# GpSimd writes one column of a spare tile between every two gathers, in the attention stage and in the last stage of a graph network

## The chip, the cores and the metric

The kernel runs on one core of one Trainium2 chip. The metric is the device time of one execution in microseconds (us), lower is better. The chip's profiler gives one further, profiled execution, from which every row below comes. Short names of the engines, as the rows have them: PE is TensorE (matmuls; PEld is its weight load), DVE is VectorE, ACT is ScalarE, POOL is GpSimd, SP is SyncE.

## What is computed

The input is 6,250 nodes with 256 features and a list of 106,250 edges (source, destination) sorted by destination. The reference has two layers. Each has a graph part, a linear attention part and an expert part:

```
xn = layernorm(x)
x  = x + gcn(xn, src, dst) + mix0(xn)              # layer 0
x  = x + experts0(layernorm(x))
xn = layernorm(x)
x  = x + gat(xn, edge_index) + mix1(xn)            # layer 1: graph attention, 8 heads of 32
x  = x + experts1(layernorm(x), router_edges)      # router = a small graph attention, 4 experts
```

The two parts that matter here are graph attentions. For every edge they compute

```
e     = leaky_relu(a_src[src] + a_dst[dst])
ex    = exp(e - m[dst])
out   = segment_sum(ex * h[src], dst) / segment_sum(ex, dst)
```

In the first (the attention stage) h has 8 heads of 32 columns. In the second (the router of the last stage) h has 4 heads of 4 columns, and the edge list has 131,072 entries. The router's result picks 2 of 4 experts for each node; each expert is a 256 to 512 to 256 network with a GELU, weighted by the gate.

## The kernel before, in words

Nodes stand 128 to a window, 49 windows (W). Edges stand 128 to a slot, sorted by window. `Stage2` (the attention stage, from line 2286) works through 880 slots of edges, `Stage3` (the last stage, from line 2934) through 1,072. Both take the slots in groups of four (GROUP): 220 groups and 268 groups. All loops are unrolled; each engine has its own hand-written program (`sync`, `pool`, `tensor`, `scalar`, `vector`), and semaphores tie them together.

For one group q the work is:

- **GpSimd** (`pool`, lines 2430 and 3101) issues four gathers (lines 2438 and 3108). One gather is an indirect DMA that fetches 128 rows of a table in HBM, one for each edge of the slot: rows of 264 float32 in the attention stage, of 20 float32 in the last stage. They land in the buffer `rows`, which has room for 8 groups in the attention stage and for 10 in the last stage (ROWS). Before it fills a buffer again, GpSimd waits until that buffer's group is used up: in the attention stage for the four matmuls of the group eight back (`s_sum`), in the last stage for the split of the group ten back (`s_part`, raised by DVE at line 3306). GpSimd has nothing else to do in either stage.
- **SyncE** loads the destinations of the group, spread over the partitions (`st_bc`).
- **ACT** makes a transposed one-hot matrix of the destinations (lines 2551 and 2555; 3191 and 3195), and the exponentials (lines 2573, 2574; 3202).
- **PE** multiplies the one-hot matrix with the window's `a_dst` (lines 2457 and 3127, into `st_pad`), and later the one-hot matrix with the weighted rows (lines 2468 and 3138, into `st_po`). These last matmuls are the segment sums.
- **DVE** adds `a_src` and `a_dst` (lines 2637 to 2647; 3279 to 3289), makes the one-hot matrix (2626; 3268), adds the four segment sums to the window's sum (line 2678; line 3314), and weights the gathered rows (line 2655; line 3298). In the last stage it also splits the weighted rows into three bf16 parts (lines 3303 to 3306).

DVE's order in a group is: exponents of group q+2, one-hot of group q+5, the four additions of group q, message of group q+2. PE's order is: the sums of group q, then a share of other dense work, then the scores of group q+3. The dense work of the attention stage is the keys, values and output of the linear attention; that of the last stage is the experts, which a planner (`plan`) spreads over groups 23 to 261. DVE takes the experts' results from PSUM at lines 3381 and 3394.

An earlier stage, `Stage1`, gathers in the same way (line 1455) and is not changed. Small `memset`s on GpSimd stand at the program's start, and one directly behind the last gather of the stage before `Stage1` (line 1016, in `block_mask`).

Of the kernel before, what the change touches and what calls it, by code (L numbers as in the profile page):

```python
# [15 lines left out]
P = 128  # L16
# [43 lines left out]
class Phase:  # L60


    def __init__(self, nc, tag, side="left"):
        self.nc, self.tag, self.ctx, self.sems, self.side = nc, tag, ExitStack(), [], side
# [194 lines left out]
class Prelude:  # L259
# [110 lines left out]
    def pool(self, g):  # L370
        for q in range(self.GROUPS):
            b = q % self.ROWS
            if q >= self.ROWS:
                g.wait_ge(self.s_sum, q - self.ROWS + 1)
            for u in range(GROUP):
                t = GROUP * q + u
                g.indirect_dma_start(self.rows[:, b, u, :], None, self.R.tab0,
                                     bass.IndirectOffsetOnAxis(self.R.gsrc[:, t:t + 1], 0)).then_inc(self.s_rows[b], 16)
        block_mask(g, Steps(g, self.s_mask), self.R.ahead.diag, HC0)
# [634 lines left out]
def block_mask(g, st, tile, width):  # L1014

    st.then(g.memset(tile[:, :], 1.0))
    v = tile[:, :].rearrange("p (g e) -> p g e", e=width)
    n = P // width
    st.then(g.affine_select(out=v, in_=v, compare_op=ALU.is_ge, fill=0.0, base=0,
                            pattern=[[-width, n], [0, width]], channel_multiplier=1))  # L1020
    st.then(g.affine_select(out=v, in_=v, compare_op=ALU.is_ge, fill=0.0, base=width - 1,
                            pattern=[[width, n], [0, width]], channel_multiplier=-1))
# [1263 lines left out]
class Stage2:  # L2286
# [32 lines left out]
    def __init__(self, f, nc, R, A):  # L2319
        self.nc, self.R, self.A = nc, R, A  # L2320
        self.wkv = self.weights(R)
        at = C * self.KV
        self.rows = self.store(R, at, self.ROWS * GROUP * GROW).rearrange("p (b u d) -> p b u d", b=self.ROWS, u=GROUP)
        at += self.ROWS * GROUP * GROW
        self.kc = self.store(R, at, 2 * self.KV).rearrange("p (k n) -> p k n", k=2)
        at += 2 * self.KV
        assert at <= C * NP
        K = self.PAIRS
        old = self.wkv.rearrange("p c n -> p (c n)")
        self.wqt = old[:, 0:K * D].rearrange("p (k d) -> p k d", k=K)  # L2330
        self.wout = old[:, K * D:2 * K * D].rearrange("p (k d) -> p k d", k=K)
        old = self.kc.rearrange("p k n -> p (k n)")
        self.m1 = old[:, 0:K * D]
        self.bd = old[:, K * D:K * D + K * P].rearrange("p (k e) -> p k e", k=K)
        self.kvsum = old[:, K * D + K * P:K * D + 2 * K * P]
        assert 2 * K * D <= C * self.KV and K * D + 2 * K * P <= 2 * self.KV
        self.diag = f.sb("diag", [P, P])
        self.xtb = f.sb("xtb", [P, self.XTB, C, P])
        self.sq = f.sb("sq", [P, 2 * W * GH + 2 * HC1])
        self.square = self.sq[:, 2 * W * GH:].rearrange("p (k e) -> p k e", k=2)  # L2340
        self.hotb = f.sb("hotb", [P, self.HOTB, P, GROUP], BF16)
        self.bc = f.sb("bc", [P, self.BCB, GROUP * P], BF16)
        self.pcol = f.sb("pcol", [P, 2])
        self.far = f.sb("far", [P, 2, GROUP * P], BF16)
        self.count = f.sb("count", [P, P, GROUP], BF16)
        self.hott = f.sb("hott", [P, self.HOTT, GROUP, P], BF16)
        self.hot = f.sb("hot", [P, self.HOTF, GROUP, P])
        self.adl = f.sb("adl", [P, W, PARTS, 2 * GH], BF16)
        self.zd = f.sb("zd", [P, GROUP, 2 * GH])
        self.z = f.sb("z", [P, 2, GROUP, 2, GH])  # L2350
        self.lm = self.sq[:, 0:W * GH].rearrange("p (w h) -> p w h", h=GH)
        self.d = f.sb("d", [P, 2, GROUP, GH])
        self.z0 = self.sq[:, W * GH:2 * W * GH].rearrange("p (w h) -> p w h", h=GH)
        self.ssum = f.sb("ssum", [P, 2, 2, HEADS])
        self.var = f.sb("var", [P, HEADS])
        self.std = f.sb("std", [P, HEADS])
        self.rs = f.sb("rs", [P, HEADS])
        self.po = f.ps("po", [P, self.BANKS, 512])
        self.pkv = f.ps("pkv", [P, 512])
        self.pacc = f.ps("pacc", [P, 512])  # L2360
        self.pad = f.ps("pad", [P, GROUP, PARTS, 2 * GH])
        self.wps = f.ps("wps", [P, GROUP, GH])
        self.zero = f.sb("zero", [P, 512], BF16)
        self.brow = f.sb("brow", [2, D])
        self.s_st, self.s_count, self.s_lm, self.s_d0, self.s_e0, self.s_a0, self.s_zero = (
            f.sem(n) for n in ("st", "count", "lm", "d0", "e0", "a0", "zero"))
        self.s_rows = [f.sem(f"rows{b}") for b in range(self.ROWS)]
        self.s_bc = [f.sem(f"bc{b}") for b in range(self.BCB)]
        self.s_hot, self.s_tt, self.s_hb, self.s_ad, self.s_z, self.s_d, self.s_ex, self.s_msg = (
            f.sem(n) for n in ("hot", "tt", "hb", "ad", "z", "d", "ex", "msg"))  # L2370
        self.s_zd, self.s_far, self.s_col = (f.sem(n) for n in ("zd", "far", "col"))
        self.s_sum, self.s_acc = f.sem("sum"), f.sem("acc")
        self.s_fw, self.s_mask, self.s_kvs, self.s_bd, self.s_pm, self.s_m1, self.s_pw = (
            f.sem(n) for n in ("fw", "mask", "kvs", "bd", "pm", "m1", "pw"))
        self.s_weff, self.s_row, self.s_mix, self.s_mixed = (f.sem(n) for n in ("weff", "row", "mix", "mixed"))
        self.s_xt = [f.sem(f"xt{k}") for k in range(self.XTB)]
        self.s_kvp, self.s_kc, self.s_sq, self.s_var, self.s_std, self.s_k1, self.s_kv = (
            f.sem(n) for n in ("kvp", "kc", "sq", "var", "std", "k1", "kv"))
# [51 lines left out]
    def pool(self, g):  # L2430
        block_mask(g, Steps(g, self.s_mask), self.diag, HC1)
        for q in range(self.GROUPS):
            b = q % self.ROWS
            if q >= self.ROWS:
                g.wait_ge(self.s_sum, GROUP * (q - self.ROWS + 1))
            for u in range(GROUP):
                t = GROUP * q + u
                g.indirect_dma_start(self.rows[:, b, u, :], None, self.R.tab1,  # L2438
                                     bass.IndirectOffsetOnAxis(self.R.gsrc[:, t:t + 1], 0)).then_inc(self.s_rows[b], 16)

# [493 lines left out]
class Stage3:  # L2934
# [24 lines left out]
    def __init__(self, f, nc, R, A, out):  # L2959
# [37 lines left out]
            f.sem(n) for n in ("st", "count", "lm", "d0", "e0", "a0", "bias"))  # L2997
        self.s_rows = [f.sem(f"rows{b}") for b in range(self.ROWS)]
        self.s_bc = [f.sem(f"bc{b}") for b in range(self.BCB)]
        self.s_far, self.s_col = f.sem("far"), f.sem("col")  # L3000
        self.s_hot, self.s_tt, self.s_ad, self.s_zd, self.s_z, self.s_d, self.s_ex, self.s_msg, self.s_part = (
            f.sem(n) for n in ("hot", "tt", "ad", "zd", "z", "d", "ex", "msg", "part"))
# [98 lines left out]
    def pool(self, g):  # L3101
        for q in range(self.GROUPS):
            b = q % self.ROWS
            if q >= self.ROWS:
                g.wait_ge(self.s_part, q - self.ROWS + 1)
            for u in range(GROUP):
                t = GROUP * q + u
                g.indirect_dma_start(self.rows[:, b, u, :], None, self.R.tabr,  # L3108
                                     bass.IndirectOffsetOnAxis(self.R.rsrc[:, t:t + 1], 0)).then_inc(self.s_rows[b], 16)

# [534 lines left out]
```

## Time and profile before

| | us |
|---|---|
| three executions without the profiler | 4553.6, 4543.36, 4551.01 |
| their median | 4551.01 |
| the profiled execution, first to last instruction (the span) | 5387.9 |
| first gather of the attention stage to its last | 2100.2 to 3425.3 |
| first gather of the last stage to its last | 3545.5 to 5314.5 |

The page gives no other time of the profiled execution than its span. It is 837 us longer than the median of the executions without the profiler. Busy time is the time in which an engine executes; "idle before" is time in which it stood still before instructions of a group, with the one that released it. Where the trace finds no instruction as releaser it writes "issue", "remote", or the name of some DMA.

### The profile page before, as it was taken

What the parts mean: (1) busy time and instruction counts of PE and PEld (TensorE: products, weight loads), DVE (VectorE), ACT (ScalarE), POOL (GpSimd) and SP (SyncE); (2) the same over time, 40 slices, a digit from 0 to 9 for tenths busy, and PEclk for the clock granted to TensorE, in tenths of its full rate; (3) what the DMA queues carried; (4) which work ended last, traced back from release to release, by engine and by line L of the source; (5) the groups of instructions that cost most, each with busy time, mean ns of one, the idle gap of its engine ahead of it and who ended that gap; (6) DMA issues with size and microseconds to landing.
All of it is one profiled execution on the core that took longest, in us unless ns stands there. A gap on an engine that the chain in (4) does not pass through costs nothing. (4 is left out here: it accounts for less than half of the span.)

```text
span 5387.9 us, 67250 instructions
## 1 busy us (share of the span) xinstructions
PE 3828.0 (71%) x17777; PEld 2450.6 (45%) x17779; DVE 3145.7 (58%) x10032; ACT 2409.6 (45%) x5559; POOL 2781.9 (52%) x2880
## 2 busy tenths in 40 slices
PE   7587789889888995676777678522666666666663
PEld 7444455556555653344444445421433333333342
DVE  7564556454454655776767767734555555555556
ACT  6232222223222333787877633323444544444444
POOL 0362656565554103666666666446555555555552
PEclk9997999999999997989888888655788788787877
DMA  2322111111111005444444455231111111111111
GB/s 91 75 71 82 40 31 41 28 39 38 29 37 24 10 31 142 115 122 117 119 118 120 125 136 136 78 83 28 30 30 31 29 31 30 30 28 29 30 30 23
DMA packets 291737, 331.29 MB, mean 61 GB/s; under 512 B 80182, under 2 KB 246062, under 8 KB 291366
## 3 DMA queue, kind: packets, MB, share of 16 engines
q0 software_dynamic: 105328, 175.77, 15.2%
q1 hardware_dynamic: 186038, 151.23, 10.1%
q8 instruction: 153, 2.51, 0.2%
q14 instruction: 218, 1.79, 0.1%
HBM read 289.56 MB, written 30.77 MB: 59 GB/s over the span
## 5 line engine op out<-in xcount | busy, mean ns | idle before, releaser
L3108 POOL DMA_INDIRECT st_rows<-tabr,router_rsrc x1072 | 1022.6, 954 | 750.6 <-DVE st_part L3306 447.8
L2438 POOL DMA_INDIRECT all_XT<-tab,graph_gsrc x880 | 843.7, 959 | 482.6 <-issue 236.7
L1455 POOL DMA_INDIRECT st_rows<-tab,graph_gsrc x748 | 735.1, 983 | 570.1 <-PE st_pe L1478 299.1
L2468 PE MATMUL st_po<-all_XT,st_hot 128*128 128x264 f32 x1760 | 569.8, 471 | 152.8 <-issue 85.7
L1704 ACT ACTIVATE st_h<-st_ph,st_shift,st_scale 128x448 f32<-128x448 f32 x448 | 320.7, 724 | 733.7 <-PE st_ph L1566 519.9
L3165 PE MATMUL st_py<-st_w,st_hid 128*128 128x256 f32 x1568 | 527.2, 489 | 55.0 <-issue 50.9
L3127 PE MATMUL st_pad<-st_adr,st_hott 128*128 x1072 | 68.8, 177 | 678.7 <-DVE st_zd L3279 536.6
L2678 DVE TENSOR_TENSOR gat_sum<-gat_sum,st_po 128x264 f32 x880 | 376.2, 428 | 200.4 <-remote 79.6
L2468 PEld LDWEIGHTS st_po<-all_XT,st_hot 128*128 128x128 f32 x1760 | 343.7, 222 | 293.1 <-issue 200.0
L3165 PEld LDWEIGHTS st_py<-st_w,st_hid 128*128 128x128 f32 x1568 | 367.4, 247 | 124.2 <-issue 59.1
L3153 PE MATMUL st_px<-all_XT,st_w 128*128 128x512 f32 (+2 forms) x832 | 406.1, 635 | 18.3 <-ACT st_hid L3213 12.9
L3202 ACT ACTIVATE st_rows<-st_d 128x16 f32<-128x16 f32 x268 | 57.9, 216 | 785.2 <-DVE st_d L3289 603.2
L3127 PEld LDWEIGHTS st_pad<-st_adr,st_hott 128*128 128x128 bf16 x1072 | 51.2, 100 | 778.6 <-issue 771.1
L1579 PE MATMUL st_po<-all_XT,st_h 128*128 128x256 f32 x1568 | 374.9, 387 | 14.5 <-DVE all_X L1895 5.1
L1566 PE MATMUL st_ph<-st_h,all_XT 128*128 128x448 f32 x896 | 372.8, 566 | 13.5 <-ACT st_h L1704 11.8
L1566 PE MATMUL st_ph<-st_xt,all_XT 128*128 128x448 f32 x896 | 367.0, 560 | 18.5 <-ACT st_h L1704 17.4
L3314 DVE TENSOR_TENSOR router_racc<-router_racc,st_po 128x60 f32 x1072 | 230.4, 215 | 225.2 <-DMA all_XT<-in_m_wout 144.7
L1791 DVE TENSOR_TENSOR gcn_acc<-gcn_acc,st_pe 128x65 f32 x748 | 166.2, 222 | 332.5 <-PE st_pe L1478 223.7
L1579 PEld LDWEIGHTS st_po<-all_XT,st_h 128*128 128x128 f32 x1568 | 292.2, 192 | 68.1 <-issue 23.8
L2655 DVE TENSOR_TENSOR all_XT<-all_XT,st_wps 128x1024 f32<-128x1024 f32 x220 | 267.3, 1215 | 22.3 <-remote 21.5
L1895 DVE SCALAR_TENSOR_TENSOR all_X<-st_po,st_gate,all_X 128x256 f32 x392 | 169.5, 478 | 143.5 <-PE st_po L1579 89.7
L1566 PEld LDWEIGHTS st_ph<-st_h,all_XT 128*128 128x128 f32 x896 | 175.6, 201 | 168.9 <-issue 140.8
(517 smaller groups left out, 7453.3 us busy)
## 6 DMA issues: line engine op xcount, KB each, us to landing
st_bc<-drowr SPq DMA_DIRECT2D x268, 128.0 KB
st_bc<-drow SPq DMA_DIRECT2D x220, 128.0 KB
st_rows<-tabr,router_rsrc POOLq DMA_INDIRECT x1072
all_XT<-tab,graph_gsrc POOLq DMA_INDIRECT x880
st_xtb<-xtd SPq DMA_DIRECT2D x98, 128.0 KB
st_rows<-tab,graph_gsrc POOLq DMA_INDIRECT x748
tab<-gat_sum SPq DMA_DIRECT2D x7, 924.0 KB
xtd<-all_XT SPq DMA_DIRECT2D x49, 128.0 KB, 1.7
```

The lines of the kernel that those rows point to most:

```text
L1455: g.indirect_dma_start(self.rows[:, b, u, :], None, self.R.tab0, bass.IndirectOffsetOnAxis(self.R.gsrc[:, t:t + 1], 0)).then_inc(self.s_ro ...
L1566: mm = t.matmul(self.ph[:, m % 3, 0:HALF], (self.w1, self.w2)[l][:, e, i, fb * P:(fb + 1) * P], src[:, i, h * HALF:(h + 1) * HALF], start= ...
L1579: mm = t.matmul(self.po[:, q % 2, j - 2 * k, :], self.h2[:, i, j * P:(j + 1) * P], self.wo[:, e, i, :], start=(i == 0), stop=(i == C - 1))
L1704: a.activation((self.h1, self.h2)[l][:, fb, h * HALF:(h + 1) * HALF], self.ph[:, m % 3, 0:HALF], ACT.Relu, bias=self.shift[:, l, i:i + 1], ...
L2438: g.indirect_dma_start(self.rows[:, b, u, :], None, self.R.tab1, bass.IndirectOffsetOnAxis(self.R.gsrc[:, t:t + 1], 0)).then_inc(self.s_ro ...
L2468: t.matmul(self.po[:, m % self.BANKS, 0:GROW], self.hot[:, q % self.HOTF, u], self.rows[:, q % self.ROWS, u, :], start=True, stop=True).th ...
L2655: v.tensor_tensor(m, m, self.wps[:, :, :].unsqueeze(3).to_broadcast([P, GROUP, GH, GC]), ALU.mult)\
L2678: v.tensor_tensor(aw, aw, self.po[:, (GROUP * q + u) % self.BANKS, 0:GROW], ALU.add).then_inc(self.s_acc, 1)
L3108: g.indirect_dma_start(self.rows[:, b, u, :], None, self.R.tabr, bass.IndirectOffsetOnAxis(self.R.rsrc[:, t:t + 1], 0)).then_inc(self.s_ro ...
L3153: mm = t.matmul(self.px[:, i, 0:n * P], self.w1[:, e, c, fb * P:(fb + 1) * P], R.XT[:, c, r * P:(r + n) * P], start=(c == 0), stop=(c == C ...
L3165: t.matmul(self.py[:, m % 2, 0:D], self.hid[:, (E1 * u + e) % 2, fb, j * P:(j + 1) * P], self.w2[:, e, fb, :], start=(fb == 0), stop=False)
L3314: v.tensor_tensor(aw, aw, self.po[:, q % self.SUMB, u * n:(u + 1) * n], ALU.add).then_inc(self.s_acc, 1)
```

## The change

A tile `rest` of 128 partitions by 2 float32 and a semaphore `s_rest` are added to both stages. Before every gather but the first of its stage GpSimd writes zero into column 0 of `rest` and raises `s_rest`; from the second of these on it first waits until the one before has raised the semaphore. Nothing reads `rest`. `Stage2` has 879 of these writes, `Stage3` has 1,071.

```diff
@@ Stage2.__init__
+        self.rest = f.sb("rest", [P, 2])
+        self.s_rest = f.sem("rest")
@@ Stage2.pool
             for u in range(GROUP):
                 t = GROUP * q + u
+                if t:
+                    if t > 1:
+                        g.wait_ge(self.s_rest, t - 1)
+                    g.memset(self.rest[:, 0:1], 0.0).then_inc(self.s_rest, 1)
                 g.indirect_dma_start(self.rows[:, b, u, :], None, self.R.tab1,
                                      bass.IndirectOffsetOnAxis(self.R.gsrc[:, t:t + 1], 0)).then_inc(self.s_rows[b], 16)
@@ Stage3.__init__
+        self.rest = f.sb("rest", [P, 2])
+        self.s_rest = f.sem("rest")
@@ Stage3.pool
             for u in range(GROUP):
                 t = GROUP * q + u
+                if t:
+                    if t > 1:
+                        g.wait_ge(self.s_rest, t - 1)
+                    g.memset(self.rest[:, 0:1], 0.0).then_inc(self.s_rest, 1)
                 g.indirect_dma_start(self.rows[:, b, u, :], None, self.R.tabr,
                                      bass.IndirectOffsetOnAxis(self.R.rsrc[:, t:t + 1], 0)).then_inc(self.s_rows[b], 16)
```

## Rows read from the trace of the kernel before

**Rows 1.** The page's head: span, then busy time of each engine.

```profile
span 5387.9 us, 67250 instructions
PE 3828.0 (71%) x17777; PEld 2450.6 (45%) x17779; DVE 3145.7 (58%) x10032; ACT 2409.6 (45%) x5559; POOL 2781.9 (52%) x2880
```

**Rows 2.** Busy time by stretch: first the attention stage, then the last stage.

```profile
core 0: us, PE busy (x) PEld busy (x) DVE busy (x) ACT busy (x) POOL busy (x), PEclk, DMA share, GB/s
2100.00:3430.00 1330.00, 940.60 (x3683) 571.52 (x3684) 927.99 (x2254) 868.76 (x2899) 843.75 (x880) 0.85 0.46 122
3545.00:5330.00 1785.00, 1042.75 (x4677) 626.99 (x4678) 947.22 (x4096) 826.50 (x1245) 1022.60 (x1072) 0.77 0.18 32
```

**Rows 3.** GpSimd's groups by line, the two that the change touches.

```profile
L3108 POOL DMA_INDIRECT st_rows<-tabr,router_rsrc x1072 | 1022.6, 954 | 750.6 <-DVE st_part L3306 447.8 <-issue 299.6 <-POOLq L73 3.2
L2438 POOL DMA_INDIRECT all_XT<-tab,graph_gsrc x880 | 843.7, 959 | 482.6 <-issue 236.7 <-remote 144.3 <-PE st_po L2468 101.3
```

**Rows 4.** GpSimd's waits over the run: us in total, times, longest us.

```profile
POOL st_rows L3108 <- DVE st_part L3306: 447.8, 110, 8.9
POOL st_rows L3108 <- issue: 299.6, 961, 1.1
...
POOL all_XT L2438 <- issue: 236.7, 758, 2.0
POOL all_XT L2438 <- remote: 144.3, 72, 3.1
POOL all_XT L2438 <- PE st_po L2468: 101.3, 49, 5.5
```

**Rows 5.** Timeline of the last stage, 4474 to 4483: start, us, engine, line.

```profile
4474.86 0.94 POOL L3108 DMA_INDIRECT st_rows<-tabr,router_rsrc  x1 [0.30 <-issue]
4476.11 0.95 POOL L3108 DMA_INDIRECT st_rows<-tabr,router_rsrc  x1 [0.31 <-issue]
4477.36 0.95 POOL L3108 DMA_INDIRECT st_rows<-tabr,router_rsrc  x1 [0.30 <-issue]
4478.68 0.97 DVE L3314 TENSOR_TENSOR router_racc<-router_racc,st_po 128x60 f32 x4 [5.55 <-DMA all_XT<-in_m_wout]
...
4482.22 0.24 DVE L3306 TENSOR_TENSOR st_part<-st_rows,st_part 128x80 bf16<-128x80 f32 x1
...
4482.73 0.95 POOL L3108 DMA_INDIRECT st_rows<-tabr,router_rsrc  x1 [4.43 <-DVE st_part L3306]
```

**Rows 6.** The two gather lines: shortest, median and longest in ns; who waited for them.

```profile
L2438 POOL DMA_INDIRECT all_XT<-tab,graph_gsrc x880: 943/949/1684, 2100.2 to 3425.3; - x176
  DVE st_z L2641: 0.5, 1
...
L3108 POOL DMA_INDIRECT st_rows<-tabr,router_rsrc x1072: 942/947/1699, 3545.5 to 5314.5; - x179
  DVE st_z L3283: 6.1, 2
```

**Rows 7.** DVE's waits in the attention stage, 2100 to 3430: in total, times, longest.

```profile
DVE st_zd L2637 <- DMA xtd<-tab_xt: 80.4, 17, 17.5
DVE gat_sum L2678 <- remote: 79.6, 46, 3.5
DVE gat_sum L2678 <- PE st_po L2468: 39.9, 31, 2.9
DVE all_XT L2655 <- remote: 21.5, 13, 2.8
```

**Rows 8.** DVE's waits in the last stage, 3545 to 5330.

```profile
DVE router_racc L3314 <- DMA all_XT<-in_m_wout: 144.7, 31, 7.5
DVE all_XT L3394 <- DMA st_brow<-in_m_bout: 134.5, 34, 6.9
DVE st_zd L3279 <- remote: 102.3, 22, 9.4
DVE all_X L3381 <- DMA st_brow<-in_m_bout: 69.4, 17, 6.9
DVE router_racc L3314 <- DMA tab<-front_tabt: 21.9, 6, 4.3
```

**Rows 9.** GpSimd's timeline, small writes at the program's start.

```profile
0.32 0.10 POOL L3635 MEMSET const-float32-0.0<- 128x1 f32 x1 [0.32 <-issue]
0.35 0.10 POOL L3635 MEMSET const-float32-1.0<- 128x1 f32 x1
0.38 0.10 POOL L3635 MEMSET const-bfloat16-1.0<- 128x1 bf16 x1
0.41 0.10 POOL L3635 MEMSET const-uint8-127<- 128x1 uint8 x1
...
9.43 0.21 POOL L137 MEMSET all_ones<- 128x128 f32 x1
9.69 0.14 POOL L139 MEMSET all_mask<- 128x49 f32 x1
```

**Rows 10.** GpSimd's timeline, a write directly behind a gather.

```profile
420.43 0.94 POOL L377 DMA_INDIRECT pre_rows<-tab,graph_gsrc  x1 [0.30 <-issue]
421.37 0.23 POOL L1016 MEMSET fold_diag<- 128x128 f32 x1
```

**Rows 11.** GpSimd's timeline, a gather behind another operation.

```profile
2099.48 0.39 POOL L1021 TENSOR_SCALAR_AFFINE_SELECT st_diag<-st_diag 128x128 f32<-128x128 f32 x1
...
2100.17 1.37 POOL L2438 DMA_INDIRECT all_XT<-tab,graph_gsrc  x1 [0.30 <-POOL st_diag L1021]
2101.84 0.95 POOL L2438 DMA_INDIRECT all_XT<-tab,graph_gsrc  x1 [0.30 <-issue]
```

## The prediction

> **What bounds the kernel now.** I read the page's head first: no engine is busy all the time, PE leads with 71% and GpSimd stands at 52% [rows 1]. That is an average over unlike stages, so the next view is busy time by stretch, for the two stages that are changed. The busiest engines are PE and DVE in the attention stage (941 and 928 us of 1330), PE and GpSimd in the last (1043 and 1023 of 1785) [rows 2]. GpSimd's share has to be read with care, because a gather costs more than its busy time. Inside a run of gathers they start 1.25 us apart (4474.86, 4476.11, 4477.36), 0.95 us busy and 0.30 us of "issue" [rows 5], and 961 of 1072 and 758 of 880 gathers have such a gap and no other [rows 4]. The gathers alone therefore fill
>
> - attention stage: 880 x 1.25 = 1100 us of the 1325 from first to last gather [rows 6];
> - last stage: 1072 x 1.25 = 1340 us of 1769 [rows 6].
>
> What is left is real waiting for a free buffer: 144.3 + 101.3 = 246 us in the attention stage, 448 us in the last [rows 3, 4]. In the profiled execution GpSimd is thus ahead of its consumers in both stages, and hardly anyone waits for a gather: 0.5 us and 6.1 us in all [rows 6].
>
> What makes the consumers slow there? The timeline shows one case: DVE stands for 5.55 us before line 3314, then the split at 3306 frees a buffer, and GpSimd, which had to wait 4.43 us, goes on [rows 5]. The view of DVE's waits collects these: 80.4 + 79.6 + 39.9 + 21.5 = 221 us in the attention stage [rows 7], 144.7 + 134.5 + 102.3 + 69.4 + 21.9 = 473 us in the last [rows 8]. All but 39.9 us of it has no believable releaser ("remote", or a DMA long done).
>
> **Profiled and timed execution.** This is the choice on which my number rests. The span is 5387.9 us and the median of the runs is 4551, so 837 us are in the profiled execution alone. DVE's unexplained waits of these two stages are 221 + 473 = 694 us, near enough to suspect that they are most of it. A gather's 1.25 us, in contrast, is the same in both stages and all but free of spread (median 949 and 947 ns, shortest 943 and 942) [rows 6], so I take it as the price without the profiler too. Two bounds for a timed run then follow.
>
> - (a) Time shrinks evenly, by 4551 / 5387.9 = 0.845: attention stage 1325 x 0.845 = 1120, last stage 1769 x 0.845 = 1495. GpSimd's slack is 1120 - 1100 = 20 us and 1495 - 1340 = 155 us.
> - (b) The unexplained waits go: 1325 - 221 = 1104 and 1769 - 473 = 1296, the latter lifted to GpSimd's 1340. Slack 4 us and 0.
>
> In both, most of the slack that the profile shows is not there in the time that counts.
>
> **The change, part by part.** Nothing is removed or moved. Added on GpSimd are 879 and 1071 writes of 128x1, each with an increment, and all but the first with a wait. No DMA is added, and no other engine has new work.
>
> *The wait* is for the write before the previous gather. GpSimd executes in order, so it is long done. Cost nothing; where the wait for a free buffer stands ahead of it, two waits come together, once in four gathers, and I cost that at nothing too, since it passes in the 0.30 us before a gather.
>
> *The write.* A 128x1 write takes 0.10 us [rows 9]. The trace has one write directly behind a gather: the gather starts at 420.43, lasts 0.94, and the write starts at 421.37, so no gap arises behind a gather [rows 10]. And it has a gather behind another operation: it starts 0.30 us after the end, as between two gathers [rows 11]. So the 0.30 us belongs to the gather that follows and isn't paid twice. The start spacing becomes 1.25 + 0.10 = 1.35 us. Bounds: at least 0.03 us, the spacing at which the four first writes start [rows 9] (the write would then run inside the 0.30 us), and below that nothing; at most the write, the 0.05 us that lie between dependent operations (9.43 + 0.21 to 9.69 [rows 9]), widened to 0.07, and a second 0.30 us, 0.47 in all. I take 0.10, because the rows of both neighbours (behind a gather, before a gather) are here.
>
> *The sum.* GpSimd needs 880 x 1.35 = 1188 us and 1072 x 1.35 = 1447 us.
>
> - By (a): 1188 - 1120 = +68 in the attention stage; 1447 is below 1495, +0. Sum +68.
> - By (b): 1188 - 1104 = +84; 1447 - 1340 = +107. Sum +191.
>
> I take the middle, +130: **4551 + 130 = 4681 us**. Against the profiled execution the same writes are 88 + 107 us, less than its slack of 246 + 448, so its span should grow little (under 60 us). The profile will show less than the timed runs do.
>
> *A rule against the row.* The write at 421.37 starts no earlier than its gather's end [rows 10], which is why I charge it in full. The Trainium skill (GPSIMD Engine Reference, section Instruction dispatch) says that completion doesn't hold back the next instruction: each of the eight cores starts it when its own share of the one before is done; and the same page says that two of the cores generate a DMA's descriptors. By that, six cores would write under the running gather, and two would still have it behind it. The rival "nearly free" below is what this would give; the row at 421.37 doesn't bear it out.
>
> **The rivals.**
>
> *Nearly free write.* The write runs inside the 0.30 us before the gather, 0.03 us each [rows 9]. GpSimd needs 880 x 1.28 = 1126 and 1072 x 1.28 = 1372: +6 by (a), +22 + 32 = +54 by (b). Middle +30: 4581. For it: small writes overlap in [rows 9]. Against: nothing shows a gather's 0.30 us overlapping with anything, 0.30 stands after a gather and after another operation alike [rows 11].
>
> *Hidden.* The slack of the profile (246 and 448 us [rows 4]) is there in the timed run too: 88 and 107 us vanish in it, 4551. That needs the 837 us to be spread where GpSimd doesn't mind, or a gather that takes less than 1.25 us without the profiler (at 1.10, even (b) hides the write in the last stage: 1072 x 1.20 = 1286 under 1296). For it: nobody waits for a gather in the trace [rows 6]. Against: slack of 246 of 1325 us isn't compatible with a run that is 15% shorter, unless the earlier stages lose nearly all of the 837.
>
> *Faster.* The waits of DVE have no named releaser. If they are no artefact, but PE's or a transfer's trouble with bursts of gathers, pacing the bursts shortens them. One eighth of the 694 us of [rows 7, 8] would be -87 us: 4464. It decides only while GpSimd has slack, and it must win more than the +68 to +191. Against: the waits are longer in the last stage, where DMA is busy 18% and a gather brings 128 rows of 80 bytes, 10 KB, than in the attention stage with 46% [rows 2]; contention would be the other way round. The gathers themselves aren't stretched either (medians 6 ns over the shortest).
>
> *Dear write.* The two-sided gap, 0.47 us a write: 880 x 1.72 = 1514 and 1072 x 1.72 = 1844. By (a) +394 + 349 = +743, by (b) +914. Around 5380. Against: [rows 10], no gap behind a gather.
>
> **How the numbers follow.** Forecast (0.10 us charged, GpSimd the bound in one or both stages) 0.50; nearly free 0.17; hidden 0.13; faster 0.12; dear 0.08. A measurement of this kernel can tell about 0.2%, 9 us, from no change. Same: all of hidden, and 0.04 of nearly free, where (a) gives 6 us: 0.17. Slower: 0.50 + 0.13 + 0.08 = 0.71. Faster 0.12. The forecast's own range is 4619 to 4742 by (a) and (b), and with a write of 0.17 us (the 0.07 included) up to 880 x 1.42 - 1104 + 1072 x 1.42 - 1340 = +328, 4879. The range takes this in at the top and hidden at the bottom, less the runs' own spread of 10 us: 4540 to 4880. Left out are faster and dear, together 0.20.
>
> **What would show it.** Right: a MEMSET row x879 and x1071 at about 100 ns; gathers in a run start 1.35 us apart, and still show 0.30 us of "issue"; GpSimd's waits for line 3306 and for 2468/"remote" shrink by about 107 and 88 us; the profiled span grows by far less than the median of the runs. Wrong: a start spacing of 1.28 or less (nearly free) or over 1.5 (dear); an unchanged median with 1.35 us spacing (the timed run has slack, hidden); DVE's unexplained waits under 600 us in sum (faster). If DVE begins to wait for gathers at line 2641 or 3283, the bound moved as forecast, only later.

## The result: 9 us slower, 0.24%

| | us |
|---|---|
| before, median of 11 runs | 4548.4 (4540.4 to 4554.0) |
| changed, median of 11 runs | 4557.6 (4551.7 to 4567.5) |
| ratio changed / before | 1.0024, 95% interval 1.0016 to 1.0033 |
| forecast | 4681, range 4540 to 4880 |

The direction was right and the size was not: +9 us in place of +130. The profile that stands ahead of the prediction, with its span of 5387.9 us, was of a disturbed execution; a later profile of the same kernel (first experiment) has a span of 4555.5, and two traces are compared below with that later one, unless [rows] are named.

### The profile after

The page's head of the changed kernel, beside [rows 1]:

```profile
span 4554.6 us, 69670 instructions
PE 3600.4 (79%) x17777; PEld 2306.1 (51%) x17779; DVE 3141.2 (69%) x10032; ACT 2406.9 (53%) x5559; POOL 3010.5 (66%) x4830
```

DVE and ACT have the busy time of [rows 1] within 5 us, but the span is 833 us shorter. PE was busy 228 us less, and GpSimd 229 us more, which are the new writes. So what went between the two profiles was mostly standing still. It has nothing to do with the edit: the later profile of the unchanged kernel is as short.

The changed kernel's chain that ended last (the instructions that held up the end, followed back from the last one), by engine and by line:

```profile
POOL 23%; issue 5%; DVE 1%; ACT 0%; PE 0%; DVEq 0%; POOLq 0%; DMA 0%
POOL st_rows L3120 21%; POOL st_rest L3119 3%; DVE router_racc L3326 0%; DVE all_X L3393 0%; PE st_px L3165 0%; PE st_py L3177 0%; ACT st_far L3203 0%; DVE st_rows L3316 0%; POOLq L3118 0%; DVE st_zd L3291 0%; DVE st_part L3318 0%; ACT L3225 0%; DVE st_part L3315 0%; DMA st_rows<-tabr,router_rsrc 0%; DVE st_part L3317 0%
```

As far back as the chain goes it runs through GpSimd: gathers, the new writes and the issue time between them. GpSimd's groups of the changed kernel, those of [rows 3] and the two new ones:

```profile
L3120 POOL DMA_INDIRECT st_rows<-tabr,router_rsrc x1072 | 1030.2, 961 | 213.1 <-issue 159.7 <-POOL st_rest L3119 48.2 <-POOLq L73 3.5
L2444 POOL DMA_INDIRECT all_XT<-tab,graph_gsrc x880 | 843.1, 958 | 175.3 <-issue 134.5 <-POOL st_rest L2443 40.5 <-POOL st_diag L1021 0.3
...
L3119 POOL MEMSET st_rest<- 128x1 f32 x1071 | 126.3, 118 | 0.4
L2443 POOL MEMSET st_rest<- 128x1 f32 x879 | 103.3, 118 | 0.2
```

The 448 and 246 us of waiting for a free buffer of [rows 3] are gone (without the edit too, as the first experiment shows), and only short gaps are left. The write takes 118 ns. A stretch of GpSimd's timeline, attention stage of the changed kernel:

```profile
2072.49 0.95 POOL L2444 DMA_INDIRECT all_XT<-tab,graph_gsrc  x1 [0.19 <-issue]
2073.44 0.11 POOL L2443 MEMSET st_rest<- 128x1 f32 x1
2073.74 0.95 POOL L2444 DMA_INDIRECT all_XT<-tab,graph_gsrc  x1 [0.19 <-POOL st_rest L2443]
2074.68 0.12 POOL L2443 MEMSET st_rest<- 128x1 f32 x1
2074.99 0.94 POOL L2444 DMA_INDIRECT all_XT<-tab,graph_gsrc  x1 [0.19 <-issue]
2075.93 0.12 POOL L2443 MEMSET st_rest<- 128x1 f32 x1
2077.02 0.95 POOL L2444 DMA_INDIRECT all_XT<-tab,graph_gsrc  x1 [0.97 <-issue]
```

Two things are to be seen. From gather to gather it is still 1.25 us (2072.49, 2073.74, 2074.99), where I had forecast 1.35: the write sits in the 0.30 us that stood between two gathers anyway, and 0.19 us of it are left behind the write. And the last gather starts 0.97 us after its write, not 0.19: it is 0.78 us late. That happens rarely, 21 times in the two stages, and it accounts for what the two stages grew by (the sum is below).

### The profile page after: what moved, and what is told of

Same layout as the page of the kernel before. It is cut to its first block and busy times, and to the rows that moved or that the text cites. A ratio compares the mean times of both kernels' runs of the same rounds, so it can differ in the third digit from the quotient of the medians.

```text
span 4554.6 us, 69670 instructions
## 1 busy us (share of the span) xinstructions
PE 3600.4 (79%) x17777; PEld 2306.1 (51%) x17779; DVE 3141.2 (69%) x10032; ACT 2406.9 (53%) x5559; POOL 3010.5 (66%) x4830
## 5 line engine op out<-in xcount | busy, mean ns | idle before, releaser
L2474 PE MATMUL st_po<-all_XT,st_hot 128*128 128x264 f32 x1760 | 518.5, 441 | 112.6 <-DVE gat_sum L2684 109.8
L3177 PE MATMUL st_py<-st_w,st_hid 128*128 128x256 f32 x1568 | 442.8, 431 | 2.1 <-ACT st_hid L3225 2.1
L2474 PEld LDWEIGHTS st_po<-all_XT,st_hot 128*128 128x128 f32 x1760 | 299.9, 202 | 255.7 <-issue 119.4
L3165 PE MATMUL st_px<-all_XT,st_w 128*128 128x512 f32 (+2 forms) x832 | 390.3, 615 | 15.8 <-ACT st_hid L3225 15.8
L3177 PEld LDWEIGHTS st_py<-st_w,st_hid 128*128 128x128 f32 x1568 | 317.8, 214 | 51.1 <-issue 3.5
```

Of the source, the lines that this page charges most:

```text
L2474: t.matmul(self.po[:, m % self.BANKS, 0:GROW], self.hot[:, q % self.HOTF, u], self.rows[:, q % self.ROWS, u, :], start=True, stop=True).th ...
L3165: mm = t.matmul(self.px[:, i, 0:n * P], self.w1[:, e, c, fb * P:(fb + 1) * P], R.XT[:, c, r * P:(r + n) * P], start=(c == 0), stop=(c == C ...
L3177: t.matmul(self.py[:, m % 2, 0:D], self.hid[:, (E1 * u + e) % 2, fb, j * P:(j + 1) * P], self.w2[:, e, fb, :], start=(fb == 0), stop=False)
```

## The experiments

### The kernel before once more; each stage alone; writes of growing width

No edit in the first run:

> The kernel before, unchanged, once more, for a second profile and for the noise. Theory N (the long profiled execution was a disturbed one): the span comes out near 4550 us, DVE's waits without a named releaser in the two stages fall from 694 us to under 100, and GpSimd's gathers start 1.25 us apart nearly throughout, 1100 us in the attention stage and 1340 in the last. Theory K (the kernel before itself suffers under the profiler, and the writes between the gathers cure it): the span is again over 5200 us. Ratio of the timed runs 1.000 under both.

Measured: 4550.1 against 4551.4 us, ratio 1.000 (0.9991 to 1.0009). The page's head, GpSimd's two groups, and who waited for the gathers (the views of [rows 3] and [rows 6]):

```profile
span 4555.5 us, 67250 instructions
...
L3108 POOL DMA_INDIRECT st_rows<-tabr,router_rsrc x1072 | 1032.9, 964 | 330.0 <-issue 316.7 <-DVE st_part L3306 9.8 <-POOLq L73 3.6
...
L2438 POOL DMA_INDIRECT all_XT<-tab,graph_gsrc x880 | 845.1, 960 | 268.0 <-issue 235.4 <-PE st_po L2468 32.3 <-POOL st_diag L1021 0.3
...
L2438 POOL DMA_INDIRECT all_XT<-tab,graph_gsrc x880: 942/946/1693, 1940.3 to 3052.2; - x176
  DVE st_z L2641: 59.5, 60
...
L3108 POOL DMA_INDIRECT st_rows<-tabr,router_rsrc x1072: 940/944/1231, 3158.0 to 4516.4; - x179
  DVE st_z L3283: 109.4, 80
```

Theory N holds and K falls. Without any edit the span is 4555.5 us, and DVE's waits in the two stages have no row left with "remote" or with a long-done DMA as releaser (694 us with the 39.9 of PE in [rows 7, 8]). The stages take 3052.2 - 1940.3 = 1111.9 and 4516.4 - 3158.0 = 1358.4 us, where 1.25 us a gather make 1100 and 1340. DVE now waits for gathers, 59.5 and 109.4 us (0.5 and 6.1 in [rows 6]). The waits on a buffer that this view still names (32.3 and 9.8 us, 0.30 each) are the usual gap ahead of a gather. GpSimd is the bound of both stages; the runs with two writes and with fewer gathers, below, test this.

The next two have the writes in one stage only:

> The 879 writes of the attention stage alone. The change as a whole cost 9 us. If each write costs a little on GpSimd's path (9 us over 1950 writes, 5 ns each), this gives +4 us (ratio 1.0009); if the price sits in one stage only, it is +9 or 0.

> The 1071 writes of the last stage alone. Evenly spread: +5 us (1.0011); if the price sits in one stage only, +9 or 0.

Measured: attention stage alone 4558.7 us, ratio 1.0015 (1.0006 to 1.0024); last stage alone 4557.9 us, 1.0015 (1.0005 to 1.0024). Both intervals lie above 1, so both stages contribute, and "one stage only" falls. More they don't tell: each interval overlaps that of the whole change (1.0016 to 1.0033), and the two rises, 7.3 and 6.5 us, add up to more than its 9.3.

The fourth widens the write from quarter to quarter of a stage:

```diff
-        self.rest = f.sb("rest", [P, 2])
+        self.rest = f.sb("rest", [P, 512])        # last stage: 128
-                    g.memset(self.rest[:, 0:1], 0.0).then_inc(self.s_rest, 1)
+                    g.memset(self.rest[:, 0:(1, 128, 256, 512)[q // 55]], 0.0).then_inc(self.s_rest, 1)
```

(in the last stage `(1, 32, 64, 128)[q // 67]`)

> The writes get wider from quarter to quarter of a stage: 1, 128, 256, 512 columns in the attention stage, 1, 32, 64, 128 in the last. From the two widths in the trace of before (49 columns 0.142 us, 128 columns 0.205) a write should take about 0.12, 0.21, 0.31, 0.52 us. Theory A (the write runs inside the 0.30 us that GpSimd needs ahead of each gather anyway): spacing of gathers 1.25, 1.25, about 1.26, 1.47. Theory B (0.19 us always lie between the write's end and the gather, and 0.12 is what happens to fit): 1.25, 1.34, 1.45, 1.66. Theory C (my forecast: write plus full 0.30): 1.35 already at one column, which the trace of the changed kernel has ruled out.

GpSimd's timeline at 128, 256 and 512 columns:

```profile
2299.88 0.95 POOL L2444 DMA_INDIRECT all_XT<-tab,graph_gsrc  x1 [0.17 <-issue]
2300.83 0.22 POOL L2443 MEMSET st_rest<- 128x128 f32 x1
2301.21 0.95 POOL L2444 DMA_INDIRECT all_XT<-tab,graph_gsrc  x1 [0.17 <-POOL st_rest L2443]
...
2600.27 0.95 POOL L2444 DMA_INDIRECT all_XT<-tab,graph_gsrc  x1 [0.17 <-issue]
2601.21 0.33 POOL L2443 MEMSET st_rest<- 128x256 f32 x1
2601.71 0.95 POOL L2444 DMA_INDIRECT all_XT<-tab,graph_gsrc  x1 [0.17 <-POOL st_rest L2443]
...
3020.85 0.95 POOL L2444 DMA_INDIRECT all_XT<-tab,graph_gsrc  x1 [0.17 <-issue]
3021.79 0.55 POOL L2443 MEMSET st_rest<- 128x512 f32 x1
3022.50 0.95 POOL L2444 DMA_INDIRECT all_XT<-tab,graph_gsrc  x1 [0.17 <-issue]
```

The medians over each quarter, worked out from the start times of all gathers in it:

| columns | write, us | end of write to gather, us | start to start, us |
|---|---|---|---|
| 1 | 0.117 | 0.191 | 1.251 |
| 32 (last stage) | 0.143 | 0.166 | 1.254 |
| 64 (last stage) | 0.166 | 0.156 | 1.272 |
| 128 | 0.218 | 0.165 | 1.336 |
| 256 | 0.326 | 0.165 | 1.443 |
| 512 | 0.539 | 0.165 | 1.656 |

The spacings are those of theory B within 0.01 us, but with about 0.165 us behind the write where it had 0.19. As a rule for these gathers: one starts 0.30 us after the end of the gather before it or about 0.165 us after the end of a write in between (0.156 to 0.166 in the medians of the wider writes, 0.14 to 0.15 behind two writes, below), whichever is later. So some 0.14 us of other work between two gathers are free, and what is beyond them costs its full time. A one-column write at 0.118 us is just under that. The spacing from start to start stands by itself; how it is split into write and gap rests on the durations that the profile reports. The kernel as a whole took 4736.6 us (a single run), 185 more than before; the two stages grew by 153.5 and 29.3 us, 183 together.

### Two writes, half the writes, fewer waits

```diff
# two
-                if t:
-                    if t > 1:
-                        g.wait_ge(self.s_rest, t - 1)
+                for k in range(2 if t else 0):
+                    if 2 * t + k > 2:
+                        g.wait_ge(self.s_rest, 2 * t + k - 2)
                     g.memset(self.rest[:, 0:1], 0.0).then_inc(self.s_rest, 1)
```

> Two writes before each gather, the second waiting for the first. Theory B of the ladder (a gather starts 0.165 us after the last write's end, and at the earliest 0.30 us after the last gather's end) with 0.118 us a write: the spacing is 0.946 + 2 x 0.118 + 0.165 = 1.35 us, or 1.42 if 0.07 us lie between the two dependent writes. If GpSimd is the bound of both stages without any slack, the median rises by 1950 times the difference to 1.25: by 195 us (4746) to 330 us (4880). If the two stages had slack as the first profile showed (246 and 448 us), it stays under 4600.

Measured: 4781.4 us against 4548.4, ratio 1.0517 (1.0501 to 1.0533), +233 us. First to last gather of the two stages, and the write's row in the last stage:

```profile
L2444 POOL DMA_INDIRECT all_XT<-tab,graph_gsrc x880: 944/945/1597, 1933.7 to 3159.8; - x176
...
L3120 POOL DMA_INDIRECT st_rows<-tabr,router_rsrc x1072: 942/943/1588, 3265.2 to 4742.7; - x179
...
L3119 POOL MEMSET st_rest<- 128x1 f32 x2142 | 229.3, 107 | 62.6
```

The stages take 1226.1 and 1477.5 us, 114 + 119 = 233 more than in the kernel before. That is the whole rise of the median: what the second write added to the stages, its time beyond the free 0.14 us and longer late gathers (below), reached the end. The median spacing is 1.364 and 1.357 us, near the lower of the two values expected. With the slack of the first profile the time would have stayed under 4600.

```diff
# half
-                if t:
+                if u % 2:
                     if t > 1:
-                        g.wait_ge(self.s_rest, t - 1)
+                        g.wait_ge(self.s_rest, t // 2)
```

> A write only before the second and fourth gather of a group. In the changed kernel one gather in 88 (attention stage) and one in 80 (last stage) starts 0.78 and about 0.5 us late, 21 times in all, 13 us; the kernel before has no such gap. Theory P (one such gap for so many instructions that GpSimd executes; the trace counts 198 and 180 between two): with 7 instead of 9 a group the gaps are about 113 and 103 gathers apart, 17 in all, and the median is +7 us (1.0015). Theory W (one for so many writes): 176 and 160 gathers apart, 10 in all, +4 us. Theory T (one for so much time): unchanged at 88 and 80.

```diff
# quad
-        self.rest = f.sb("rest", [P, 2])
+        self.rest = f.sb("rest", [P, 4])
+                if u == 1 and t > 1:
+                    g.wait_ge(self.s_rest, t - 1)
                 if t:
-                    if t > 1:
-                        g.wait_ge(self.s_rest, t - 1)
-                    g.memset(self.rest[:, 0:1], 0.0).then_inc(self.s_rest, 1)
+                    g.memset(self.rest[:, u:u + 1], 0.0).then_inc(self.s_rest, 1)
```

> As many writes as in the changed kernel, but into four columns, with a single wait for earlier writes in a group, placed before the second gather so that it never meets the wait for a free buffer. If the small cost comes from the waits, the gaps of 0.78 and 0.5 us go and the ratio is 1.000. Theory P (instructions executed; 8 a group instead of 9): gaps about 99 and 90 gathers apart, ratio 1.002. Theory W and T: unchanged at 88 and 80.

Measured: half the writes 4551.9 us, ratio 1.0007 (0.9998 to 1.0016); fewer waits 4553.3 us, ratio 1.0009 (1.0000 to 1.0018). The late gathers, from the gaps in front of all gathers (a gather counts as late when its gap is over 0.08 us above the median gap; with half the writes, gathers with a write in front, usually 0.191 us, and without one, 0.305, were taken each by themselves). Gathers of a stage are counted from 0, so "behind 112" means that gather 113 is the late one, always the second of its group:

| kernel | attention stage | last stage |
|---|---|---|
| before | none | none |
| changed | 9, 0.78 us each, behind gather 112, 200, ... 816 | 12, 0.28 to 0.56 us, behind 112, 192, ... 992 |
| attention stage alone | 9, 0.78 us, same places | none |
| last stage alone | none | 12, 0.19 to 0.55 us, same places |
| two writes | 9, 1.27 us, same places | 12, 1.13 to 1.18 us, same places |
| growing width | 7 in the same places: 0.78 us at 1 column, 0.63 at 128, 0.42 at 256; none at 512 | 12, same places: 0.55 us at 1 column, 0.52 to 0.57 at 32, 0.30 to 0.54 at 64, 0.39 to 0.42 at 128 |
| half the writes (gather 113 and the like have one in front) | none | none |
| fewer waits | 9, 0.13 us, same places | none |

The same place in the kernel with fewer waits, 0.32 us in front where 0.19 is usual:

```profile
2084.20 0.95 POOL L2444 DMA_INDIRECT all_XT<-tab,graph_gsrc  x1 [0.19 <-issue]
2085.15 0.11 POOL L2443 MEMSET st_rest<- 128x1 f32 x1
2085.58 0.94 POOL L2444 DMA_INDIRECT all_XT<-tab,graph_gsrc  x1 [0.32 <-issue]
```

And with two writes, where a usual gap stands in front of 2090.56, 0.15 us behind the writes:

```profile
2090.14 0.27 POOL L2443 MEMSET st_rest<- 128x1 f32 x2
2090.56 0.94 POOL L2444 DMA_INDIRECT all_XT<-tab,graph_gsrc  x1
2091.50 0.27 POOL L2443 MEMSET st_rest<- 128x1 f32 x2
2093.19 0.94 POOL L2444 DMA_INDIRECT all_XT<-tab,graph_gsrc  x1 [1.42 <-issue]
```

All three theories that I had written down fall. The places don't follow the number of instructions (P), of writes (W) or the time (T: with two writes it takes 9% longer to gather 112, and still that one it is). They follow the number of gathers, or of groups (no run tells these two apart): first behind gather 112, then every 88 in the attention stage and every 80 in the last. What follows the writes and waits is the size: nothing at two writes a group, 0.13 and nothing at four writes with one wait, 0.78 and 0.55 at four writes with four waits, 1.27 and 1.18 at eight. The expectation on the waits (fewer of them, and the gaps go) came nearest, but waits alone don't order the runs: two a group, with two writes, gave nothing, and one, with four writes, 0.13. And the size falls as the write gets wider, from 0.78 to 0.42 us and to nothing at 512 columns. That would fit a fixed piece of work that comes up every 80 or 88 gathers and is hidden when there is time enough for each of GpSimd's instructions. It isn't shown: no row names such work. A load of program code isn't it, as far as the trace tells: the DMA view of the changed kernel from 2071 to 2077 us, up to the late gather above, has no packet of the kind "instruction", nor has the last microsecond before any of the nine late ones of that stage. What it is stays open.

### Fewer gathers, and the changed kernel once more

```diff
 # the kernel before
             for u in range(GROUP):
                 t = GROUP * q + u
+                if u == 3 and q >= self.ROWS:
+                    continue
                 g.indirect_dma_start(self.rows[:, b, u, :], None, ...
-            v.wait_ge(self.s_rows[b], 16 * GROUP * (q // self.ROWS + 1))
+            v.wait_ge(self.s_rows[b], 16 * GROUP + 48 * (q // self.ROWS))
```

> The kernel before without the fourth gather of each group from the buffer's second use on: 212 gathers fewer in the attention stage, 258 fewer in the last stage (the old rows of the buffer are used in their place, so the output is not the reference's). It asks how far below GpSimd the next engine is. The gathers then need 668 x 1.25 = 835 us and 814 x 1.25 = 1018 us. Theory G (GpSimd alone holds both stages at 1112 and 1358 us, and DVE, with its 1007 and 1123 us of work and small gaps, is next): the stages come out near 1040 to 1080 and 1150 to 1250 us, and the median falls by 150 to 280 us. Theory D (the consumers need as much as GpSimd, and only keep pace with it by accident): the median falls by less than 50 us.

Measured: 4413.3 us against 4548.8, ratio 0.9703 (0.9687 to 0.9719), -135 us. GpSimd's groups and the stages' times:

```profile
L3112 POOL DMA_INDIRECT st_rows<-tabr,router_rsrc x814 | 772.9, 949 | 468.9 <-DVE st_part L3310 271.4 <-issue 193.8 <-POOLq L73 3.7
...
L2440 POOL DMA_INDIRECT all_XT<-tab,graph_gsrc x668 | 636.9, 953 | 404.3 <-PE st_po L2470 257.2 <-issue 146.8 <-POOL st_diag L1021 0.3
...
L2440 POOL DMA_INDIRECT all_XT<-tab,graph_gsrc x668: 940/946/1707, 1933.1 to 2973.1; - x167
...
L3112 POOL DMA_INDIRECT st_rows<-tabr,router_rsrc x814: 938/944/1742, 3095.5 to 4332.7; - x163
```

The stages' gathers now take 1040 and 1237 us, and GpSimd waits for buffers again, 257 and 271 us. So with a quarter fewer gathers the consumers are the bound, some 6% and 9% below where GpSimd holds the kernel before. That is near what theory G expected (1040 to 1080 and 1150 to 1250 us), and D falls. The median falls by less than these 193 us together, because the consumers trail the last gather by more: from the last gather to the end it is 4406.4 - 4332.7 = 74 us, against 4555.5 - 4516.4 = 39 before, and between the stages 122 against 106. The fall of 135 us is 15 short of the 150 to 280 that theory G gave, and far above D's 50.

> The changed kernel once more, for a second profile. If the late gathers are fixed to their place in the order, they are again those after gather 112, 200, 288 and so on of the attention stage (every 88) and after 112, 192, 272 and so on of the last (every 80), 0.78 and about 0.55 us late.

The second profile of the changed kernel (span 4561.9 us, a single run) has the late gathers in the same 21 places, 0.78 us in the attention stage and 0.19 to 0.56 us in the last.

## Why the prediction was right in direction and wrong in size

- **GpSimd bounds both stages in the time that counts: right.** Bound (b), 1104 and 1340 us, is near the measured 1112 and 1358; bound (a), 1120 and 1495, was far off in the last stage. The inference (DVE's unexplained waits belong to that one execution, a gather's 1.25 us doesn't) was sound. My reason for it, that the profiler takes the 837 us, was wrong: later profiles of the same kernel and of its variants have spans within 3 us of that run's own time. Two of the numbers were not quite: the 694 us hold 39.9 that do have a releaser, so 654 are unexplained; and the 246 and 448 us of waiting hold the usual 0.30 us of each wait, which 1.25 us a gather counts already (1100 + 246 is more than the 1325 of the stage). The slack of that profile was 1325 - 1100 = 225 and 1769 - 1340 = 429 us.
- **"So the 0.30 us belongs to the gather that follows and isn't paid twice. The start spacing becomes 1.25 + 0.10 = 1.35 us": wrong.** This is the step that failed; the spacing measured is 1.251 and 1.249 us. The first half is true: nothing is paid twice. But the 0.30 us overlap with what stands between the gathers, up to 0.14 us of it, and the write's 0.10 us, charged in full 1950 times, cost nothing there. I leaned on [rows 11], where a gather follows another operation by 0.30 us. There the kernel makes GpSimd wait for that operation (every step of the mask ends in a wait), so the row shows a gather behind a wait, not one behind a free-running write. The row had a wait in it that the edit's code has not in this place. That the wait makes the difference is argued and not tested, as no run puts a wait between a write and its gather. In its favour: a gather that waited for another engine starts 0.27 us after that one's end, in [rows 5] (4482.46 to 4482.73) and in the median of 142 such gathers of the last stage in the run with fewer gathers.
- **The price of the write, 0.10 us: measured 0.118**, and no gap behind the gather, as [rows 10] had it. What the usual write adds to the path is 0.
- **"The wait costs nothing": true for the spacing, not for the rare gather.** Where two waits come together the spacing stays 1.25 us. But the late gathers of the attention stage are 0.78 us late with a wait at every write and 0.13 with one in a group.
- **The sum.** In place of +68 to +191 the stages grew by 1117.0 - 1111.9 = 5.1 and 1361.8 - 1358.4 = 3.4 us. The late gathers make 9 x 0.78 = 7.0 and 12 in the last stage 6.2 us; single gathers that ran longer than the median make 1.9 and 2.8 us less than before. That is 8.5 us, near the median's 9.3. The spans of these two profiled executions differ by less than 1 us all the same, because the attention stage began 8.4 us earlier in the changed kernel; its start varies from 1931.5 to 1943.0 us over the ten later profiles. The stages' own times are steadier: 1117.0 to 1117.8 us with the writes in three profiles and 1111.9 and 1112.5 without any in two, 1361.8 to 1364.2 and 1354.7 to 1358.4 in the last stage.
- **The direction was right by luck.** The forecast's mechanism, a longer spacing, added nothing. By the profiles the 9 us come from rare late gathers, which no term of the sum has and whose cause is open. The time also lies inside the range, but in the part that was put there for "hidden", which needed slack that wasn't there. And taking the middle of (a) and (b) made the miss smaller: by (b), the better bound, it would have been +191.
- **The rivals.** "Nearly free write" has the mechanism (the write inside the 0.30 us) and its sign, a start spacing of 1.28 us or less, came true; I had its price at 0.03 us a gather, and it is 0, so its 4581 was 23 us too high. "Hidden", with 4551, has the nearer time and the wrong reason: there was no slack, as two writes show. "Dear" is out by the spacing. "Faster" is out too, though its sign (under 600 us of unexplained waits) came: these waits were gone without the edit.
- **The profiled span** should have grown by under 60 us; it fell by 833, because the first one was disturbed. The comparison said nothing. The same holds for the waits for a free buffer, which should have shrunk by 107 and 88 us: in an undisturbed execution there were none to shrink.
- **The rule of the Trainium skill** (GPSIMD Engine Reference, Instruction dispatch: completion of an instruction doesn't hold back the next). I wrote that a row didn't bear it out. Of cores that work under a running gather nothing can be seen here either: the write starts at 2073.44, when the gather of 2072.49 ends. The overlap is between the write and the gather that follows: the gather comes 0.165 us after a write and not 0.30, so part of those 0.30 us passes beside the write.

## What to carry to other kernels

Between two back-to-back gathers on GpSimd there were 0.30 us, and 0.14 us of them could be used by a small operation at no cost to the usual gather; beyond that these two stages, bound by GpSimd, paid in full, 233 us for a second 0.1 us write before every gather. A gap between two instructions is not a price that belongs to one of them: look whether the row from which you take it has a wait in it, and whether the gap is a minimum distance that other work can fill. When the profiled execution is 18% longer than the runs, take a second profile, or ask what it would look like without the unexplained waits, before reading slack from it.

## What was not expected of the hardware

- A gather of 128 rows costs GpSimd the same 1.25 us whether a row has 80 or 1056 bytes (1.249 and 1.251 us median spacing), and the DMA share of the stages is 0.27 and 0.57.
- Behind gather 112 and then every 88 (attention stage) or 80 (last stage) gathers, the next gather is late by an amount that grows with the number of writes and waits between gathers and falls with the width of the write: 0 at two writes a group, 0.78 and 0.55 us at four with a wait each, 1.27 and 1.18 us at eight; with four, 0.42 us at 256 columns and 0 at 512 (attention stage). The cause is open; an experiment that changes the number of buffers (8 and 10, which divide 88 and 80) wasn't made.
- One profiled execution of the kernel before had 5387.9 us, at equal busy time of DVE and ACT, and none of the ten later profiles was like it.

The DMA shares come from the stretches of the kernel before, second profile:

```profile
1930.00:3060.00 1130.00, 875.79 (x3732) 502.65 (x3734) 942.44 (x2297) 871.24 (x2917) 846.64 (x884) 0.94 0.57 146
3150.00:4525.00 1375.00, 948.67 (x4747) 581.71 (x4746) 966.89 (x4184) 835.16 (x1263) 1033.33 (x1073) 0.85 0.27 42
```
